# 16-head attention rebuilt on two score layouts, with stacked operands sent through DRAM

## The chip, the cores and the metric

The kernel runs on one core of a Trainium2 chip. The metric is the device time of one execution in microseconds; lower is better.

## The reference

Four layers, each an attention and a feed-forward part, on x of 16 x 256 tokens by 128. The attentions of layers 0, 2 and 3 have 16 heads of width 8 over a context of 64 rows per batch, and are what is changed:

```python
x = x + xattn(_layernorm(x), ctx)
# in xattn: q, k, v by head
scores = jnp.einsum('bhqd,bhkd->bhqk', q, k)
scores = jnp.where(mask, NEG, scores)          # layer 0: keys whose token is 0
probs = jax.nn.softmax(scores / np.sqrt(HD), axis=-1)
attn = jnp.einsum('bhqk,bhkd->bhqd', probs, v)
return attn @ Wo + bo
```

Layers 2 and 3 have a mask of query by key, which with these inputs masks nothing. Layer 1's attention has one head and is not touched.

## The kernel before, in words

Tokens lie on partitions: 32 tiles of 128 tokens, two tiles to a batch. `X` holds the residual stream in SBUF for the whole kernel, `MV` its mean and variance per token.

Before each attention a preparation (`prep_parts`, L196) computes the keys transposed, `KT`, and `VB`, the values padded with a column of ones. It is a stage of its own for layers 0 and 3; for layer 2 it runs at the end of the expert stage, just before the rows that the experts wrote are gathered back to `XH` by indirect DMAs on GpSimd (L1668) and added to `X` (L1644).

`mha` (L334) is one stage. Each engine has its own instruction list, made by `tile_slots` (L184) of one slot per tile, written out for the first and last four and in a loop of four slots between; engines meet at semaphores alone, and each executes its own list in order. In a slot:

- TensorE computes the scores of tile t+1 in two halves (`scores`, L388): queries stationary, and as moving operand `kbd`, the keys spread over 16 heads with zeros elsewhere, 512 columns a half, in f32. Between the halves it transposes the 8 chunks of the exponentials of tile t-1 (L407). Then come the transpose of the attended tile t-3 (L417), the attended values of tile t-2 (L425: 8 products with the transposed exponentials stationary and 18 columns moving) and the output projection of t-3 (L431). In layer 0 each half gets a bf16 product more, for the padding mask (L396).
- VectorE divides tile t-3 by its sums (L528, L531), and for each half of t+1 takes the maximum of each head (L518) and writes the shifted scores `Z` (L521). It adds the output of t-4 to `X` and takes its statistics (L542 to L551).
- ScalarE takes the exponential (L457), copies the transposed exponentials out of PSUM (L462) and the smaller transposes (L445, L450, L469).
- GpSimd builds `kbd` (L484) and adds the output bias (L486), once per batch.

There is no DMA within an attention stage, beyond the last of the loads that were issued earlier.

## Time and profile before

| | us |
|---|---|
| median of 3 runs | 1820.06 (1814.22 to 1820.89) |
| the profiled execution | 1815.55 |
| its span in the trace | 1813.7 |
| attention of layer 0, 35.2 to 237.5 | 202.3 |
| attention of layer 2, 989.2 to 1165.0 | 175.8 |
| attention of layer 3, 1589.3 to 1764.5 | 175.2 |
| TensorE busy | 1415.0 (78%) |
| VectorE busy | 1143.6 (63%) |
| ScalarE busy | 616.5 (34%) |
| GpSimd busy | 265.5 (15%) |

The span is what the trace covers; the execution's own time has 1.85 us more around it. The attention stages are measured from the first reciprocal of the token scales (L142) to the last statistics. A busy TensorE is one whose records follow each other without a gap; a record contains some 0.17 us in which the next has already begun. The granted clock (PEclk) is 1.00 where TensorE is granted 2.4 GHz, and 0.50 at 1.2 GHz.

### The profile page before, as it was taken

The page shows a single profiled execution, that of the slowest core. Times are in us where ns is not written, and L with a number is a line of the kernel's source. Part 1 is how long each engine was busy: PE and PEld are TensorE (multiplying, and loading weights), DVE is VectorE, ACT ScalarE, POOL GpSimd, SP SyncE. Part 2 cuts the span into 40 slices and gives each one's busy share as a digit, 9 for nine tenths or more (in the row PEclk, how much of TensorE's full clock was granted, in tenths as well). Part 3 has the DMA queues.
Part 4 walks back from the last instruction along what each step waited for, and adds up shares of the span by engine and source line. Part 5 has one row for each costly group of instructions (what it writes and reads, how often), then busy time and mean ns, then how long its engine had stood idle before and what let it go on. Part 6 is the DMA issues. An engine that isn't in the chain of part 4 may idle for free. (4 is left out here: it accounts for less than half of the span.)

```text
span 1813.7 us, 26829 instructions
## 1 busy us (share of the span) xinstructions
PE 1415.0 (78%) x7716; PEld 1061.2 (59%) x7749; DVE 1143.6 (63%) x3741; ACT 616.5 (34%) x1055; POOL 265.5 (15%) x237
## 2 busy tenths in 40 slices
PE   3999976999976663302760999699999999789982
PEld 1666665998964453201540777567777777557761
DVE  5777774576647875670243888645556655578868
ACT  1444403444433220000110555334444444345541
POOL 1222100010101100064246222000000000032202
PEclk8999986999995555555875999799999999989995
DMA  6000000000000031002321000000000000000001
GB/s 218 1 0 0 0 1 1 1 2 0 1 1 1 0 124 30 0 20 84 113 69 32 1 0 0 1 1 1 1 1 0 0 0 1 1 1 0 0 1 47
DMA packets 38579, 34.21 MB, mean 19 GB/s; under 512 B 8672, under 2 KB 35552, under 8 KB 38112
## 3 DMA queue, kind: packets, MB, share of 16 engines
q1 hardware_dynamic: 35168, 26.78, 4.9%
q0 software_dynamic: 3328, 6.43, 1.1%
q8 instruction: 39, 0.64, 0.1%
q14 instruction: 44, 0.36, 0.1%
HBM read 24.15 MB, written 9.44 MB: 19 GB/s over the span
## 5 line engine op out<-in xcount | busy, mean ns | idle before, releaser
L392 PE MATMUL mha_pS<-mha_kbd,mha_qT 128*128 128x512 f32 x384 | 203.9, 616 | 3.6 <-ACT mha_qT L450 3.4
L484 POOL TENSOR_TENSOR mha_kbd<-KT,w_ctx 128x1024 f32<-128x1024 f32 x48 | 91.2, 1901 | 758.3 <-SPq L97 460.5
L1982 DVE SCALAR_TENSOR_TENSOR tree_hl<-tree_pH,tree_hh 128x512 fp32r<-128x512 f32 x192 | 132.4, 689 | 94.8 <-ACT tree_hh L1879 93.2
L425 PEld LDWEIGHTS mha_pO<-VB,mha_PT 128*128 128x128 f32 x1536 | 183.2, 192 | 10.8 <-issue 8.7
L425 PE MATMUL mha_pO<-VB,mha_PT 128*128 (+1 forms) x1536 | 178.3, 259 | 0.0
L1879 ACT ACTIVATE tree_hh<-tree_pH 128x512 fp32r<-128x512 f32 x192 | 114.6, 597 | 146.1 <-PE tree_pH L1783 112.1
L518 DVE TENSOR_REDUCE mha_nm<-mha_pS 128x8 f32<-128x512 f32 x192 | 131.6, 686 | 44.4 <-PE mha_pS L396 24.1
L521 DVE TENSOR_TENSOR mha_Z<-mha_pS,mha_nm 128x512 f32<-128x512 f32 x192 | 132.9, 692 | 19.3
L462 ACT ACTIVATE mha_PT<-mha_pT 128x1024 f32<-128x1024 f32 x96 | 98.3, 1024 | 136.5 <-PE mha_pT L407 136.0
L457 ACT ACTIVATE mha_PR<-mha_Z 128x1024 f32<-128x1024 f32 x96 | 101.5, 1057 | 86.1 <-DVE mha_Z L521 86.0
L407 PEld LDWEIGHTS mha_pT<-w_ctx,mha_PR 128*128 128x128 f32 x768 | 87.4, 141 | 38.4 <-issue 38.2
L1796 PE MATMUL tree_pY<-tree_hh,w2h 128*128 128x512 f32 x192 | 101.0, 526 | 5.5 <-DVE tree_hl L1982 5.2
L1124 ACT ACTIVATE ffn_hid<-ffn_pH,w_ffn 128x512 f32<-128x512 f32 x128 | 85.5, 687 | 54.3 <-PE ffn_pH L1049 53.7
L407 PE MATMUL mha_pT<-w_ctx,mha_PR 128*128 128x128 f32 x768 | 101.2, 275 | 0.0
L1233 DVE SCALAR_TENSOR_TENSOR ffn_acc<-ffn_pE,ffn_wt,ffn_acc 128x128 f32<-128x128 f32 x192 | 54.1, 344 | 71.1 <-PE ffn_pE L1062 71.0
L1062 PEld LDWEIGHTS ffn_pE<-W2R,ffn_hid 128*128 128x128 f32 x768 | 93.6, 192 | 4.4
L1062 PE MATMUL ffn_pE<-W2R,ffn_hid 128*128 128x128 f32 x768 | 93.8, 275 | 0.0
L1780 PE MATMUL tree_pH<-tree_xTh,w1h 128*128 128x512 f32 x192 | 80.8, 421 | 1.0 <-DVE tree_sel L1976 1.0
L1569 PE MATMUL exp_pX<-w_ctx,exp_xe 128*128 128x128 f32 (+1 forms) x48 | 12.2, 336 | 84.5 <-DMA exp_xe<-slots_in 84.5
L1782 PE MATMUL tree_pH<-tree_xTh,w1l 128*128 128x512 f32 x192 | 76.6, 399 | 0.0
L1796 PE MATMUL tree_pY<-tree_hl,w2h 128*128 128x512 f32 x192 | 76.2, 397 | 0.0
L1781 PE MATMUL tree_pH<-tree_xTl,w1h 128*128 128x512 f32 x192 | 76.1, 396 | 0.0
(422 smaller groups left out, 2822.8 us busy)
## 6 DMA issues: line engine op xcount, KB each, us to landing
w_tree_full<-in_tree_full_dram SPq DMA_DIRECT2D x1, 4224.0 KB, 14.2
exp_W<-in_L_W_dram SPq DMA_DIRECT2D x32, 128.0 KB, 2.3
slots_in<-route_zero SPq DMA_DIRECT2D x40, 64.0 KB, 1.8
w_rot<-in_rot_dram SPq DMA_DIRECT2D x1, 2307.0 KB, 8.7
X<-in_x_dram SPq DMA_DIRECT2D x8, 256.0 KB, 5.8
exp_xe<-slots_in SPq DMA_DIRECT2D x16, 128.0 KB, 3.0
slots_out<-exp_ye POOLq DMA_DIRECT2D x16, 128.0 KB, 2.9
out_dram<-X SPq DMA_DIRECT2D x8, 256.0 KB, 2.3
```

The lines of the kernel that those rows point to most:

```text
L392: ins = pe.matmul(pS[:, n, :], qT[u][:, P * v:P * v + P], kbd[u][:, 8 * n:8 * n + 8, :], start=True, stop=not key_mask)
L407: ins = pe.transpose(pT[:, P * c:P * c + P], PR[v][:, P * c:P * c + P], ident)
L425: ins = pe.matmul(pOv[:, c, :], PT[v][:, P * c:P * c + P], VB[:, a.b(-2), c, :], start=True, stop=True)
L457: act.activation(PR[v][:], Z[v][:].rearrange("p h k -> p (h k)"), ACT.Exp, scale=HD ** -0.5).then_inc(s["P"], 1)
L462: act.activation(PT[v][:], pT[:], ACT.Copy).then_inc(s["PT"], 1)
L484: pool.tensor_tensor(kbd[u][:], kb, bmask.unsqueeze(2).to_broadcast([P, H, SK]), ALU.mult).then_inc(s["kbd"], 1)
L518: dve.tensor_reduce(mx, sc, AX.X, ALU.max, negate=True).then_inc(s["nm"], 1)
L521: dve.tensor_tensor(Z[v][:, HH * n:HH * n + HH, :], sc, mx.unsqueeze(2).to_broadcast([P, HH, SK]), ALU.add).then_inc(s["Z"], 1)
L1062: ins = pe.matmul(pE[p % 2][:, j, :], hc, core.W2R[:, P * r:P * r + P], start=(c == 0), stop=(c == 1))
L1796: ins = pe.matmul(bank[:], w2[:, k0], h[k % 2][:], start=(c == 0 and i == 0), stop=False)
L1879: act.activation(hh[k % 2][:], pH[k % 2][:], ACT.Relu).then_inc(s["h"], 1)
L1982: dve.scalar_tensor_tensor(hl[k % 2][:], pH[k % 2][:], 0.0, hh[k % 2][:], ALU.max, ALU.subtract).then_inc(s["lo"], 1)
```

## The change

Each attention computes its scores twice. In the first layout (tokens on partitions) they serve only to find the maximum of each head. In the second (keys on partitions) they are computed again with the maximum taken off inside the product, so that the exponential is taken straight out of PSUM into the layout that the attended values need. `Z`, its subtraction and the 8 transposes of the exponentials per tile are gone.

All score products are in f32r. To keep the precision, queries and keys are split into a high and a low part, stacked on partitions: in four groups of four heads, query rows high, high, low against key rows high, low, high, 32 rows each. Below these lie rows of ones, and 8 rows with the negated maxima (high and low part) of the group. The queries of four tiles (a quad) are written to DRAM as `qd` and read back stacked (2 writes and 3 reads of 256 KB each per quad, 8 quads); the maxima of a batch go the same way as `md` (32 KB each way, 16 batches). SyncE issues all of these in one list.

The attended values have `VB` stationary (18 columns) and 256 columns of exponentials moving, four products into the partitions from 0, 32, 64 and 96 of one PSUM bank, two such sets per batch. Their result is copied to `OT` and transposed back to tokens on partitions (`tokens`, 2 transposes per tile).

All slots are written out, from -8 to 44; slot t takes the scores and maximum of tile t, the second scores and exponentials of tile t-6, the attended values of t-8, the division (`rc`, `at`), transpose and projection of t-11, and the residual addition of t-12. VectorE's list takes `largest(t)` first in its slot. The normalisation of `X` moves to ScalarE. The preparation makes the stacked keys `KS` from 8 products with a copy on ScalarE and a subtraction on VectorE for each, where it had 2 products and copies; it also fills the extra rows. GpSimd spreads `KS` over the heads (`ks`), 1024 columns per batch, as it did for `kbd`.

The core of the diff (the declarations, the branch for a mask that masks something, and the packing of the inputs are left out):

```diff
+            for g in range(NQ):
+                need(pe, s_l, NQ * n + g - 1)
+                pe.matmul(pk[g % 2][0:3 * HR, :], w("wk3")[:, 3 * HR * g:3 * HR * g + 3 * HR], ctx, start=True, stop=True).then_inc(s_k, 1)
...
+            for g in range(NQ):
+                act.wait_ge(s_k, NQ * n + g + 1)
+                act.activation(KS[0:3 * HR, g, 512 * n:512 * n + 512], pk[g % 2][0:3 * HR, :], ACT.Identity,
+                               bias=w("bk3")[0:3 * HR, g:g + 1]).then_inc(s_kt, 1)
...
+        dve.memset(KS[3 * HR:last, :, :].bitcast(F32), 1.0).then_inc(s_z, 1)
         dve.memset(VB[:], 0.0).then_inc(s_z, 1)
-        dve.wait_ge(s_z, 1)
+        if key_mask:
+            dve.wait_ge(s_z, 1)
+            dve.tensor_scalar(KS[3 * HR:3 * HR + 3, :, :], core.itok[3 * HR:3 * HR + 3, :].unsqueeze(1).to_broadcast([3, NQ, B * SK]), 0.0,
+                              core.w("mha0", "neg3")[3 * HR:3 * HR + 3, :], ALU.is_equal, ALU.mult)
+        lo = slice(HR, 2 * HR)
+        for n in range(2):
+            for g in range(NQ):
+                dve.wait_ge(s_kt, NQ * n + g + 1)
+                kl = KS[lo, g, 512 * n:512 * n + 512]
+                dve.scalar_tensor_tensor(kl, pk[g % 2][lo, :], w("bk3")[lo, g:g + 1], kl, ALU.add, ALU.subtract).then_inc(s_l, 1)
+        dve.wait_ge(s_z, 2)
...
+    QB, KB, QT = 3, 4, 4
+    QS = QT * P
+    SC = HD ** -0.5
...
+        PT = [core.XH[:, 16 * u:16 * u + 16, :].rearrange("p (c t) d -> p c (t d)", c=CH) for u in range(2)]
+        OT = two("OT", [P, 2, S])
...
+        pS = st.ps("pS", [P, H, SK])
+        pST = st.ps("pST", [P, CU, S])
+        pQ, pO, pAb, pYb = (st.ps(n, [P, 512]) for n in ("pQ", "pO", "pA", "pY"))
+        pOv = pO[:].rearrange("p (r t) -> p r t", r=2)
+        pA, pV = pAb[:, 0:P], pAb[:, P:P + S]
+        pVc = pV.rearrange("p (c w) -> p c w", w=HR)
+        pY, pN = pYb[:, 0:P], pYb[0:2 * H, P:P + S]
...
+        FIRST, LAST = -8, T + 13
+        UN, AT, OE, HT = 6, 8, 10, 11
+        quad = lambda t: t // QT
...
+            def write_queries(q):
+                sp.wait_ge(s["q"], q + 1)
+                for n, src in enumerate((qh, ql)):
+                    sp.dma_start(core.qd[n, q], plain(src[:])).then_inc(s["qw"], 16)
+            def read_queries(q):
+                u = q % QB
+                sp.wait_ge(s["qw"], LW * (q + 1))
+                need(sp, s["ST"], QT * (q - QB) + QT)
+                for n, h in enumerate((0, 0, 1)):
+                    sp.dma_start(plain(qs[u][HR * n:HR * n + HR, :, :]), core.qd[h, q].rearrange("(g r) c -> r g c", g=NQ)).then_inc(s_ld[u], 16)
+            def write_shifts(b):
+                sp.wait_ge(s["nT"], b + 1)
+                sp.dma_start(core.md[b], plain(nT[b % 2][:])).then_inc(s["mw"], 16)
+            def read_shifts(b):
+                u, c0 = (b // 2) % QB, S * (b % 2)
+                sp.wait_ge(s["mw"], 16 * (b + 1))
+                need(sp, s_m[b % 2], 16 * (b // 2))
+                sp.dma_start(plain(qs[u][K0:K1, :, c0:c0 + S]), core.md[b].rearrange("(g j) c -> j g c", g=NQ)).then_inc(s_m[b % 2], 16)
+            for t in range(FIRST, LAST):
+                if not even(t) and live(t - 3):
+                    write_shifts((t - 3) // TB)
+                if t % QT == 3 and live(t + 5):
+                    write_queries(quad(t + 5))
+                if not even(t) and live(t - 3):
+                    read_shifts((t - 3) // TB)
+                if t % QT == 2 and live(t + 2):
+                    read_queries(quad(t + 2))
...
+            def scores(t):
+                b, q = t // TB, quad(t)
+                u, c0 = q % QB, P * (t % QT)
+                if t % QT == 0:
+                    pe.wait_ge(s_ld[u], LD * (q // QB + 1))
+                if even(t):
+                    pe.wait_ge(s["k"], b + 1)
+                need(pe, s["nm"], t)
+                for g in range(NQ):
+                    ins = pe.matmul(pS[:, NH * g:NH * g + NH, :], qs[u][0:KC, g, c0:c0 + P], ks[b % KB][0:KC, g, :, :],
+                                    start=True, stop=True)
                 ins.then_inc(s["S"], 1)
...
+            def shifts(b):
+                pe.wait_ge(s["nx"], b + 1)
+                need(pe, s["X"], TB * b + 2 - HT)
+                need(pe, s["nT"], b)
+                for v in range(TB):
+                    src = nx[b % 2][:, v, :, :, :].rearrange("p g n h -> p (g n h)").bitcast(F32)
+                    ins = pe.transpose(pN[:, P * v:P * v + P], src, ident)
+                ins.then_inc(s["nTp"], 1)
+            def scores_T(b, i):
+                u, c0 = (b // 2) % QB, S * (b % 2)
+                if i == 0:
+                    pe.wait_ge(s_m[b % 2], LM * (b // 2 + 1))
+                need(pe, s["P"], TB * b + i)
+                for n in range(CU):
+                    c = CU * i + n
+                    g, h0 = c // 2, 2 * (c % 2)
+                    ins = pe.matmul(pST[:, n, :], ks[b % KB][0:K1, g, h0:h0 + 2, :], qs[u][0:K1, g, c0:c0 + S], start=True, stop=True)
+                ins.then_inc(s["ST"], 1)
+            def attend(b, r):
+                if r == 0:
+                    need(pe, s["OT"], b)
+                pe.wait_ge(s["P"], TB * b + 2)
+                for j in range(4):
+                    c = 4 * r + j
+                    ins = pe.matmul(pOv[HR * j:HR * j + VW, r, :], VB[:, b, c, :], PT[b % PB][:, c, :], start=True, stop=True)
+                ins.then_inc(s["O"], 1)
+            def tokens(t):
+                b, v = divmod(t, TB)
+                pe.wait_ge(s["OT"], b + 1)
+                need(pe, s["aT"], t)
+                for r in range(2):
+                    ins = pe.transpose(pV[:, P * r:P * r + P], OT[b % 2][:, r, P * v:P * v + P], ident)
+                ins.then_inc(s["V"], 1)
+            def heads_T(t):
+                pe.wait_ge(s["at"], t + 1)
+                pe.transpose(pA, at[:], ident).then_inc(s["aTp"], 1)
+            def output(t):
+                pe.wait_ge(s["aT"], t + 1)
+                need(pe, s["X"], t)
+                need(pe, s["nT"], min(B, (t + HT) // TB))
+                pe.matmul(pY, aT[t % 2][:], w("wo"), start=True, stop=True).then_inc(s["Y"], 1)
...
+            for t in range(FIRST, LAST):
+                if live(t):
+                    scores(t)
+                if live(t - UN):
+                    scores_T((t - UN) // TB, (t - UN) % TB)
+                if live(t - HT):
+                    heads_T(t - HT)
+                if live(t - AT):
+                    attend((t - AT) // TB, (t - AT) % TB)
+                if even(t) and live(t - 2):
+                    shifts((t - 2) // TB)
+                if live(t - HT + 1):
+                    tokens(t - HT + 1)
+                if t % QT == 1 and live(t + 7):
+                    x_transposes(quad(t + 7))
+                if t % QT == 2 and live(t + 6):
+                    queries(quad(t + 6))
+                if live(t - HT):
+                    output(t - HT)
...
+            def q_evac(q):
+                act.wait_ge(s["qp"], q + 1)
+                need(act, s["qw"], LW * q)
+                act.activation(qh[:], pQ[:], ACT.Identity, bias=w("bq")).then_inc(s["qh"], 1)
+            def shifts(b):
+                act.wait_ge(s["nTp"], b + 1)
+                need(act, s["mw"], 16 * (b - 1))
+                act.activation(nT[b % 2][:], pN, ACT.Copy).then_inc(s["nT"], 1)
+            def exponentials(b, i):
+                n = TB * b + i
+                act.wait_ge(s["ST"], n + 1)
...
+                need(act, s["O"], TB * (b - PB) + 2)
+                act.activation(PT[b % PB][:, CU * i:CU * i + CU, :], pST[:], ACT.Exp, scale=SC).then_inc(s["P"], 1)
...
+            for t in range(FIRST, LAST):
+                if even(t) and live(t - OE):
+                    attended((t - OE) // TB)
+                if live(t + 10) and t + 10 >= QT:
+                    normalise(t + 10)
+                if live(t - HT):
+                    heads_T(t - HT)
+                if live(t - UN):
+                    exponentials((t - UN) // TB, (t - UN) % TB)
+                if even(t) and live(t - 2):
+                    shifts((t - 2) // TB)
+                if t % QT == 1 and live(t + 7):
+                    x_evac(quad(t + 7))
+                if t % QT == 2 and live(t + 6):
+                    q_evac(quad(t + 6))
...
+                def q_low(q):
+                    dve.wait_ge(s["qh"], q + 1)
+                    dve.scalar_tensor_tensor(ql[:], pQ[:], w("bq"), qh[:], ALU.add, ALU.subtract).then_inc(s["q"], 1)
+                def largest(t):
+                    dve.wait_ge(s["S"], t + 1)
...
+                    dve.tensor_reduce(nm[:, t, :], pS[:], AX.X, ALU.max, negate=True).then_inc(s["nm"], 1)
+                def split_shift(b):
+                    dve.wait_ge(s["nm"], TB * b + 2)
+                    need(dve, s["nTp"], b - 1)
+                    src = nm[:, TB * b:TB * b + TB, :].rearrange("p v (g h) -> p v g h", h=NH)
+                    dve.tensor_copy(nx[b % 2][:, :, :, 0, :], src).then_inc(s["nh"], 1)
+                    dve.wait_ge(s["nh"], b + 1)
+                    dve.tensor_tensor(nx[b % 2][:, :, :, 1, :], src, nx[b % 2][:, :, :, 0, :], ALU.subtract).then_inc(s["nx"], 1)
...
+                for t in range(FIRST, LAST):
+                    if live(t):
+                        largest(t)
+                    if live(t - HT):
+                        r = t - HT
+                        dve.wait_ge(s["V"], r + 1)
+                        dve.reciprocal(rc[r % 2][:], pVc[:, :, 2 * HD:VW]).then_inc(s["rc"], 1)
+                    if even(t) and live(t - 2):
+                        split_shift((t - 2) // TB)
+                    if live(t - HT):
                         need(dve, s["aTp"], r)
...
+                        dve.wait_ge(s["rc"], r + 1)
+                        dve.tensor_tensor(at[:].rearrange("p (c h d) -> p c h d", h=2, d=HD),
+                                          pVc[:, :, 0:2 * HD].rearrange("p c (h d) -> p c h d", d=HD),
+                                          rc[r % 2][:].unsqueeze(3).to_broadcast([P, CH, 2, HD]), ALU.mult).then_inc(s["at"], 1)
+                    if live(t - HT - 1):
+                        x = t - HT - 1
+                        dve.wait_ge(s["Y"], x + 1)
+                        dve.wait_ge(s["bo"], x // TB + 1)
+                        dve.tensor_tensor(X[:, x, :], pY, X[:, x, :], ALU.add).then_inc(s["X"], 1)
+                    if live(t - HT - 1):
+                        dve.wait_ge(s["X"], x + 1)
+                        dve.bn_stats(bn[x % 2][:], X[:, x, :]).then_inc(s["bn"], 1)
...
+                    if t % QT == 2 and live(t + 6):
+                        q_low(quad(t + 6))
+                    if live(t - HT - 1):
+                        dve.wait_ge(s["bn"], x + 1)
+                        dve.bn_aggr(MV[:, x, :], bn[x % 2][:])
...
+            if key_mask:
+                for u in range(QB):
+                    dve.memset(qs[u][3 * HR:K0, :, :].bitcast(F32), 1.0).then_inc(s["one"], 1)
+            dve.memset(pO[:], 0.0).then_inc(s["zero"], 1)
             rs_dve(dve)
+            dve.scalar_tensor_tensor(NB[:], MV[:, :, 0], -1.0, RS[:], ALU.mult, ALU.mult).then_inc(s["nb"], 1)
...
```

## Rows read from the trace of the kernel before

**Rows 1.** Windows over the attention stages: window, length, PE, PEld, DVE, ACT, POOL, PEclk, DMA, GB/s.

```profile
35.20:237.50 202.30, 196.13 (x1120) 128.46 (x1120) 144.06 (x357) 88.63 (x129) 39.18 (x32) 0.97 0.00 0
989.20:1165.00 175.80, 166.80 (x1056) 128.23 (x1056) 136.69 (x357) 86.32 (x130) 39.36 (x32) 0.96 0.00 0
1589.30:1764.50 175.20, 167.46 (x1056) 128.44 (x1056) 136.88 (x357) 86.46 (x130) 39.23 (x32) 0.96 0.00 0
```

**Rows 2.** Timeline in layer 3's attention, one slot and more: start us, us, instruction.

```profile
1661.14 1.02 PE L392 MATMUL mha_pS<-mha_kbd,mha_qT 128*128 128x512 f32 x2
...
1662.00 1.04 PE L407 MATMUL mha_pT<-w_ctx,mha_PR 128*128 128x128 f32 x8
...
1664.06 1.86 PE L425 MATMUL mha_pO<-VB,mha_PT 128*128 x16
...
1665.77 0.47 PE L431 MATMUL mha_pY<-w_mha,mha_aT 128*128 128x128 f32 x2
...
1666.07 1.02 PE L392 MATMUL mha_pS<-mha_kbd,mha_qT 128*128 128x512 f32 x2
...
1666.17 0.25 DVE L528 RECIPROCAL mha_rc<-mha_pO 128x16 f32<-128x16 f32 x1
...
1666.53 0.29 DVE L531 TENSOR_TENSOR mha_at<-mha_pO,mha_rc 128x128 f32<-128x128 f32 x1
...
1668.78 0.60 PE L386 MATMUL mha_pQ<-mha_xT,w_mha 128*128 128x256 f32 x2
```

**Rows 3.** Groups of instructions, layer 3's attention, 1610 to 1700: busy us, mean ns.

```profile
L518 DVE TENSOR_REDUCE mha_nm<-mha_pS 128x8 f32<-128x512 f32 x36 | 24.5, 681 | 2.2 <-PE mha_pS L392 2.2
...
L484 POOL TENSOR_TENSOR mha_kbd<-KT,w_ctx 128x1024 f32<-128x1024 f32 x10 | 19.0, 1902 | 56.4 <-PE mha_pS L392 56.4
...
L462 ACT ACTIVATE mha_PT<-mha_pT 128x1024 f32<-128x1024 f32 x18 | 18.4, 1024 | 22.8 <-PE mha_pT L407 22.8
...
L542 DVE TENSOR_TENSOR X<-mha_pY,X 128x128 f32 x17 | 4.8, 281 | 0.0
```

**Rows 4.** Timeline of TensorE in layer 2's tree stage: two f32r products.

```profile
1315.76 0.40 PE L1781 MATMUL tree_pH<-tree_xTl,w1h 128*128 128x512 f32 x1
1315.99 0.40 PE L1782 MATMUL tree_pH<-tree_xTh,w1l 128*128 128x512 f32 x1
```

**Rows 5.** Timeline at the start of layer 3's attention.

```profile
1589.80 0.19 DVE L143 TENSOR_TENSOR mha_nta<-mha_vea,RS 128x32 f32<-128x32 f32 x1
1590.02 0.19 DVE L144 TENSOR_TENSOR mha_nta<-mha_nta,RS 128x32 f32<-128x32 f32 x1
...
1591.81 0.69 PE L381 MATMUL mha_pQ<-w_ctx,mha_xh 128*128 128x128 f32 x2 [7.56 <-DVE mha_xh L501]
...
1592.97 1.22 PE L386 MATMUL mha_pQ<-mha_xT,w_mha 128*128 128x256 f32 x2 [0.47 <-ACT mha_xT L445]
```

**Rows 6.** DMA issues on the page: size of each, median us from issue to landing.

```profile
X<-in_x_dram SPq DMA_DIRECT2D x8, 256.0 KB, 5.8
...
out_dram<-X SPq DMA_DIRECT2D x8, 256.0 KB, 2.3
```

**Rows 7.** Timeline: preparation of layer 3, of layer 0, and the gather before layer 2.

```profile
1579.23 1.98 DVE L216 MEMSET VB<- 128x2304 f32 x1 [0.82 <-PEq L97]
...
1579.85 0.69 ACT L213 ACTIVATE KT<-prep_pk,w_mha 128x512 f32<-128x512 f32 x1 [3.64 <-PE prep_pk L206]
...
1581.60 0.61 DVE L227 TENSOR_TENSOR VB<-prep_pv,w_mha 64x64 f32<-64x64 f32 x4
...
14.86 0.73 DVE L292 TENSOR_SCALAR nbias<-itok,w_mha 3x1024 bf16<-3x1024 int32 x1
...
968.14 0.75 DVE L1644 TENSOR_TENSOR X<-X,XH 128x512 f32<-128x512 f32 x1 [3.73 <-DMA XH<-slots_out,slots]
```

**Rows 8.** Windows elsewhere: layer 1's attention, and the expert stage (columns as in Rows 1).

```profile
548.00:600.00 52.00, 34.74 (x104) 21.34 (x104) 41.67 (x278) 15.06 (x40) 6.52 (x9) 0.51 0.00 1
...
882.00:886.00 4.00, 1.83 (x5) 1.19 (x6) 0.57 (x2) 0.00 (x0) 1.26 (x2) 0.73 0.67 203
```

385 lines of the change are left out of this document (147 added, 238 removed).

## The prediction

> **What bounds the kernel now.** Two views say where the change can act. The windows over the three attention stages come first [rows 1]: 202.3, 175.8 and 175.2 us, 553.3 of the span's 1813.7. TensorE is busy for 95 to 97% of each at a granted clock of 0.96 to 0.97, and VectorE for 144.1, 136.7 and 136.9 us, ScalarE for half of the time. The timeline of one slot shows how tightly TensorE is packed [rows 2]: from one first half of scores (1661.14) to the next (1666.07) pass 4.93 us, in which 8 transposes (1.04), the attended values (1.86), the projection (0.47) and the two halves of scores follow each other. So before, these stages are bound by TensorE's own work: 32 slots of some 5.0 us make 160, and filling and emptying the pipeline 16. In layer 0 two mask products per tile lengthen the slot; from 202.3 - 16 it is 5.8 us.
>
> The change therefore has to be priced as a slot: what one tile costs once the new pipeline is full, and what the longer pipeline costs before and after that. All sums below are against the profiled execution, 1815.6 us; the median of the runs, 1820.1, is 4.5 above it.
>
> **The new slot, step by step.** What TensorE is spared is clear: the two halves in f32, 1.9 us of issue, and the 8 transposes. An f32r product of 512 columns starts 0.23 us before the next [rows 4]; one of 256 columns is then 0.12, and the two layouts together are 8 of these, 0.96 us. VectorE loses the subtraction into `Z`. But the order of the two lists makes a loop that the old kernel did not have. In slot t TensorE issues the scores of t, then those of t-6, and then `heads_T(t-11)`, which needs `at(t-11)`. VectorE has the sums for that from the slot before, yet its list puts `largest(t)` first, and that waits for the scores of this very slot. So TensorE stands still after its second scores until VectorE has taken the maximum and divided. Counting from the start of slot t:
> - Four score products: the last starts at 0.36 and ends 0.12 + 0.17 later, at 0.65. The 0.17 is what a record holds beyond its issue: 0.40 against 0.23 [rows 4].
> - `largest`: 512 PSUM elements take 0.68 and 128 take 0.28 [rows 3], so 1.04 ns an element, and 1024 take 1.22; I take 1.24. With 0.03 before it.
> - `rc` and `at`: `at` starts 0.36 after `rc` and takes 0.29 [rows 2], 0.65. In even slots `split_shift` stands between, two small operations that follow at 0.22 each as two such ones do [rows 5]: 0.45 in half of the slots, 0.22 in the mean.
> - With 0.07 for the hand-over, `heads_T` starts at 2.86. TensorE's second scores were issued by 0.96; it has been idle for 1.7 us.
> - From there TensorE issues: `heads_T` 0.12 (8 transposes take 1.04), attended values A, `shifts` 0.22 every second slot, `tokens` 0.24, x transposes 0.48 and queries 0.92 every fourth, the projection 0.30 (1665.77 to 1666.07) [rows 2]. That is 0.12 + 0.11 + 0.24 + 0.12 + 0.23 + 0.30 + A, 1.12 + A.
> - Two hold-ups more. `q_low` is ahead of the next `largest` on VectorE: a query product (0.92 + 0.17), its copy (0.69 for 512 columns [rows 7]) and `q_low` (0.69) end 0.8 us after the next scores would have been ready, every fourth slot: 0.20. And `output` must wait in even slots until ScalarE has copied the shifts out of the same bank, which stands behind the exponential of 1024 columns, 1.02 [rows 3]; where no query product covers that it is 0.5 us, every fourth slot: 0.12.
>
> The slot is 2.86 + 1.12 + 0.20 + 0.12 + A = 4.30 + A.
>
> **A is the open price**: four f32 products of 256 columns whose outputs lie in four different 32-partition strips, which no row shows. Bounds: one after the other each costs 0.43, from 0.60 for a product of 256 columns less 0.17 [rows 2], so A = 1.72; all four at once, A = 0.45. An f32 product is two records, and the second of a product writes where its first does. If it must wait for that and only neighbours of different products overlap, there are five steps of 0.215 where there were eight: A = 1.07. I take this one: it is the middle of the ends, and the rows are as far from both, since none of them writes part of the partitions.
>
> So the slot is 5.37 us, against 5.0 in layers 2 and 3 and 5.8 in layer 0.
>
> **Fill and drain.** Only slots 11 to 31, 21 of them, are full. Before slot 0 come normalisation, transposes, queries and their two copies at the half clock: a transposition of two is 0.69 and a product of 256 columns 1.22 [rows 5], and with 512 columns everywhere this ends at 8 us; then two writes and three reads of 256 KB. A store of that size lands in 2.3 us and a load among many in 5.8 [rows 6]; I take 3 and 5, and scores start at 16.5 us, with 10 and 20 as ends. Slots 0 to 7 are chains of scores, maximum and the next scores, 1.95 us, with 0.7 more in even slots and 2.7 more where queries come: 23 us. Slots 8 to 10 add the attended values: 10. Slot 11 begins at 50. After slot 31 there are six slots of 2.2, two of 1.8, five of 1.3 and an end of 1.3: 24.5. A layer is 50 + 21 x 5.37 + 24.5 = 187.3, three are 562, 9 more than 553.3.
>
> **Preparation.** VectorE fills `KS`: 4096 columns at the 1.98 us of 2304 [rows 7] are 3.5, before everything else. Then eight rounds of product, copy (0.69) and subtraction (0.69) over two banks: two rounds take about 2.5 us, 10 in all, less what the fills cover, and only then come the additions into `VB` (0.61 for four). Layer 3's preparation grows by 12.5. Layer 0's grows as much, its mask rows (four times 0.73) standing for the removed multiplication of `KT`, and its attention begins with three fills of 2048 columns, 5.3, of which 0.5 hides beside the table load: 4.8. For layer 2 I charge nothing: the same 12 us lie ahead of additions to `X` that each wait 3.73 us for a gather [rows 7]; seven such waits absorb them. Without that cover it would be 12.
>
> **Costed at nothing otherwise**: ScalarE has 1.02 + 0.3 + 0.3 + 0.3 + 0.5 = 2.4 us of work in a slot of 5.3. GpSimd builds 1024 columns per batch as before, 1.90 us [rows 3], in two slots. The queue of SyncE carries 1.3 MB in 21 us; the queries are asked for three slots, 15 us, before use, the shifts come back after one write and one read, 5 us, and have three slots. SyncE's list is in order: a late `q` would hold up the shifts behind it, but it is there 1.3 us into the slot.
>
> **The clock.** In a stretch of the expert stage in which TensorE was idle for over half of the time the granted clock was 0.73, and in layer 1's attention, 34.7 busy of 52, it was 0.51 [rows 8]; before it was 0.96. With 1.7 us idle in each slot I take 0.95 of what it is at 1.00 for the 2.8 us that TensorE has on the path: 63 x 2.8 / 0.95 less 63 x 2.8, 9 us.
>
> Sum: 1815.6 + 9 + 12.5 + 12.5 + 4.8 + 9 = **1863 us**. TensorE loses its work and gets a wait for VectorE instead.
>
> **The rivals.**
> - *The strips run one after the other* (A = 1.72). For it: each f32 product in the rows before, even of 18 columns, has its own 0.12 [rows 2], none overlap. Slot 6.00; 29 slots have attended values, so 3 x 29 x 0.65 = 57 more, less 1 for the smaller wait of `output`: 1919.
> - *All four strips at once* (A = 0.45), not slower than before. The slot loses 0.62, but `output` then waits on the exponential and the shift copy in every even slot, 0.33 instead of 0.12 in the mean: 4.96. Drain gives 5 us a layer. 3 x (21 x 0.41 + 5) = 41 less: 1822, no change. It decides as soon as A is below 0.5; if the fill is 5 us a layer shorter as well, 1807, and faster when measured. The Trainium skill's page "TensorE: Matmul & The Clock Gate", section "Part 3: Packing small matmuls — row/col tiling", is for it: matmuls in different column strips run concurrently, a few ns apart. By that rule the sum is the 1822 of this rival; no row of the trace has such strips.
> - *The clock stays low.* If TensorE is granted 0.5 as in layer 1's attention, its 2.8 us on the path double: slot 8.2, 3 x 21 x 2.8 = 176 less the 9 counted: 2030. For it: the stages start at half clock and each slot has a gap. Against: the old stages start at half clock too and still had 0.96 in the mean [rows 1]. It decides from a mean clock below 0.9.
> - *The order costs nothing*: `at` is ready before TensorE asks. Then the slot is TensorE's sum, 0.96 + 1.07 + 1.12 = 3.15, or VectorE's 1.24 + 0.87 + 0.03 and some 1.1 for `X`, the statistics and `q_low`, 3.3, with the hold-ups 3.6, and 3 x 21 x 1.77 = 111 go: 1752. Against it is the list itself.
>
> **How the numbers follow.** Forecast 0.40, strips in sequence 0.22, strips at once 0.20, low clock 0.08, order free 0.10. A measurement of this kernel tells from no change what is over 0.5%, 9 us. The forecast's own range, with fill at its ends (-6 to +4 a layer) and clock 0.9 to 1.0, is 1836 to 1887. Of the rival at 1822, which its fill moves either way, half is faster, as is the case of a free order, and a little of the forecast: faster 0.24. Same 0.13, from the other half; slower 0.63. The range takes in both neighbours and some error of the fill: 1795 to 1930.
>
> **What would show it.** Right: TensorE idle for about 1.7 us before `heads_T`, released by `at`; `largest` at 1.24; slots of 5.4 us; scores of slot 0 some 15 us after the token scales; preparations of about 21 us. Wrong: starts of the four strip products 0.43 apart, or 0.02 apart; a clock under 0.9; TensorE waiting on the stacked reads in the steady state; or no wait for `at` at all.

## The result, and the profile after

The kernel after takes 1901.3 us (median of four runs, 1893.8 to 1908.1) against 1820.5 for the kernel before beside it: a ratio of 1.044 (95% interval 1.039 to 1.050). Its profiled execution took 1908.1 us, the slowest of the four, with a span of 1906.1 against 1813.7. Of 92.4 us more in the span, the attention stages hold 33.4, and what comes ahead of them 56.1:

| stretch | change, us | forecast |
|---|---|---|
| start and preparation of layer 0 | +20.1 | +17.3 |
| attention of layer 0 | -10.9 | -15.0 |
| expert stages with layer 2's preparation | +20.6 | 0 |
| attention of layer 2 | +21.3 | +11.5 |
| preparation of layer 3 | +15.4 | +12.5 |
| attention of layer 3 | +23.0 | +12.1 |
| the rest | +2.9 | 0 |

(An attention runs from the reciprocal of its token scales to its last statistics. The expert row runs from the token scales of the feed-forward part behind layer 0's attention, and layer 3's preparation from those of layer 2's tree stage, each to the token scales of the attention that follows. The forecast of an attention stage is 187.3 less the old length; its 9 us for the clock stand for all three together.)

First the three attention stages, answering to [rows 1], and then the full slots alone, from the maximum of tile 11 to that of tile 31, 20 slots each. The columns are window, length, PE, PEld, DVE, ACT, POOL, PEclk, DMA, GB/s.

```profile
55.30:246.70 191.40, 131.25 (x752) 86.43 (x752) 85.80 (x238) 75.44 (x145) 37.87 (x31) 0.71 0.23 61
1019.30:1216.40 197.10, 136.10 (x752) 89.85 (x752) 85.97 (x238) 75.77 (x146) 37.83 (x31) 0.68 0.22 59
1658.20:1856.40 198.20, 139.68 (x752) 91.65 (x752) 85.84 (x238) 75.66 (x145) 37.85 (x31) 0.65 0.22 59
...
112.40:216.80 104.40, 73.09 (x456) 50.37 (x457) 49.43 (x142) 39.09 (x76) 24.48 (x20) 0.78 0.21 57
1078.70:1186.30 107.60, 77.90 (x456) 53.72 (x457) 49.40 (x141) 39.32 (x76) 24.45 (x20) 0.72 0.20 56
1714.80:1827.70 112.90, 84.26 (x456) 57.17 (x457) 49.46 (x142) 39.45 (x76) 24.50 (x20) 0.64 0.19 53
```

TensorE was busy for 95 to 97% of these stages and is now for 69 to 70%, and the granted clock fell from 0.96 or 0.97 to between 0.65 and 0.71: in long stretches TensorE is granted 1.2 GHz and not 2.4. A full slot is 5.22, 5.38 and 5.64 us, longest where the clock is lowest. One slot of layer 0 shows the loop that the prediction described:

```profile
135.29 0.33 PE L471 MATMUL mha_pA<-w_ctx,mha_at 128*128 128x128 f32 x1 [1.65 <-DVE mha_at L631]
135.55 0.63 PE L458 MATMUL mha_pO<-XH,VB 128*18 128x256 f32 x8
136.11 0.50 PE L466 MATMUL mha_pA<-w_ctx,mha_OT 128*128 128x128 f32 x2
...
136.69 1.20 PE L428 MATMUL mha_pS<-mha_ks,mha_qs 99*128 99x256 f32 x4
137.69 1.05 PE L449 MATMUL mha_pST<-mha_qs,mha_ks 107*128 107x256 f32 x4
137.93 1.23 DVE L590 TENSOR_REDUCE mha_nm<-mha_pS 128x16 f32<-128x1024 f32 x1 [1.96 <-PE mha_pS L428]
139.07 0.25 DVE L625 RECIPROCAL mha_rc<-mha_pA 128x16 f32<-128x16 f32 x1
139.50 0.28 DVE L631 TENSOR_TENSOR mha_at<-mha_pA,mha_rc 128x128 f32<-128x128 f32 x1
139.84 0.48 PE L471 MATMUL mha_pA<-w_ctx,mha_at 128*128 128x128 f32 x1 [1.09 <-DVE mha_at L631]
140.25 1.06 PE L458 MATMUL mha_pO<-XH,VB 128*18 128x256 f32 x8
```

VectorE stands still for 1.96 us until the scores are there, takes the maximum, then divides, and TensorE waits for `at` (the bracket gives the idle time and who ended it). In all TensorE waits for `at` 93.8 us in 78 of 96 slots, 1.2 us each in the mean where the forecast had it idle for 1.7. Two things differ from the forecast's slot: the four score products are 1.0 us apart in all and not 0.48, since they run at half clock, and the eight records of attended values (L458) give way to the next work 0.56 us after their first start at full clock (135.55 to 136.11) and after 0.98 at half (140.25 to 141.23), not after 1.07. In the trace's single records the first records of the four products start 0.007 us apart, and the second ones follow 0.21 us later.

Layer 2's preparation lies in the expert stage. Its row of before shows VectorE held by the gather's arrivals, 3.73 us each [rows 7]; after, it is late itself:

```profile
944.32 3.47 DVE L192 MEMSET KS<- 8x4096 f32 x1 [0.91 <-issue]
...
962.03 0.61 DVE L214 TENSOR_TENSOR VB<-exp_pX,w_mha 64x64 f32<-64x64 f32 x4
967.77 0.61 DVE L214 TENSOR_TENSOR VB<-exp_pX,w_mha 64x64 f32<-64x64 f32 x4 [5.13 <-remote]
978.32 0.61 DVE L214 TENSOR_TENSOR VB<-exp_pY,w_mha 64x64 f32<-64x64 f32 x4 [9.94 <-remote]
991.65 0.61 DVE L214 TENSOR_TENSOR VB<-exp_pY,w_mha 64x64 f32<-64x64 f32 x4 [12.72 <-remote]
...
1001.28 0.67 DVE L1742 TENSOR_TENSOR X<-X,XH 128x512 f32<-128x512 f32 x1
```

VectorE waits 27.8 us for the sixteen value products, which by TensorE's own records ran from 960.0 to 963.7, while GpSimd issues gathers from 947.2 to 988.6. The first addition to `X` comes at 1001.3, 54 us after the first gather is issued; the kernel before had it at 950.2, 11 us after the first gather.

### The profile page after: what moved, and what is told of

Same layout as the page of the kernel before. It is cut to its first block and busy times, and to the rows that moved or that the text cites. A ratio compares the mean times of both kernels' runs of the same rounds, so it can differ in the third digit from the quotient of the medians.

```text
span 1906.1 us, 22929 instructions
## 1 busy us (share of the span) xinstructions
PE 1316.9 (69%) x6776; PEld 949.0 (50%) x6809; DVE 1019.5 (53%) x3414; ACT 594.0 (31%) x1121; POOL 261.2 (14%) x237
## 5 line engine op out<-in xcount | busy, mean ns | idle before, releaser
L590 DVE TENSOR_REDUCE mha_nm<-mha_pS 128x16 f32<-128x1024 f32 x96 | 117.2, 1220 | 192.1 <-PE mha_pS L428 192.1
L568 POOL TENSOR_TENSOR mha_ks<-KS,w_ctx 104x1024 fp32r<-104x1024 f32 (+1 forms) x48 | 90.8, 1892 | 904.2 <-POOLq L99 553.2
L428 PE MATMUL mha_pS<-mha_ks,mha_qs 96*128 96x256 f32 (+1 forms) x384 | 107.6, 423 | 35.0 <-DMA mha_qs<-queries 14.1
L428 PEld LDWEIGHTS mha_pS<-mha_ks,mha_qs 96*128 96x128 f32 (+1 forms) x384 | 82.5, 291 | 53.1 <-issue 26.1
L530 ACT ACTIVATE XH<-mha_pST 128x1024 f32<-128x1024 f32 x96 | 97.9, 1020 | 14.1 <-PE mha_pST L449 13.7
L449 PE MATMUL mha_pST<-mha_qs,mha_ks 104*128 104x256 f32 (+1 forms) x384 | 82.7, 352 | 2.1 <-ACT XH L530 1.3
L458 PE MATMUL mha_pO<-XH,VB 128*18 128x256 f32 x768 | 76.5, 479 | 0.0
L449 PEld LDWEIGHTS mha_pST<-mha_qs,mha_ks 104*128 104x128 f32 (+1 forms) x384 | 73.6, 263 | 4.2 <-issue 2.3
L1894 PE MATMUL tree_pY<-tree_hh,w2l 128*128 128x512 f32 x192 | 75.2, 392 | 0.0
L471 PE MATMUL mha_pA<-w_ctx,w_top 128*128 128x128 f32 x64 | 24.3, 380 | 61.4 <-DVE w_top L631 61.4
```

What stands on the lines that cost most here:

```text
L428: ins = pe.matmul(pS[:, NH * g:NH * g + NH, :], qs[u][0:KC, g, c0:c0 + P], ks[b % KB][0:KC, g, :, :], start=True, stop=True)
L449: ins = pe.matmul(pST[:, n, :], ks[b % KB][0:K1, g, h0:h0 + 2, :], qs[u][0:K1, g, c0:c0 + S], start=True, stop=True)
L530: act.activation(PT[b % PB][:, CU * i:CU * i + CU, :], pST[:], ACT.Exp, scale=SC).then_inc(s["P"], 1)
L568: pool.tensor_tensor(ks[b % KB][0:K1, :, :, :], kb, hb, ALU.mult).then_inc(s["k"], 1)
L590: dve.tensor_reduce(nm[:, t, :], pS[:], AX.X, ALU.max, negate=True).then_inc(s["nm"], 1)
L1894: ins = pe.matmul(bank[:], w2[:, k0], h[k % 2][:], start=(c == 0 and i == 0), stop=False)
```

## The experiments

All times are medians of four runs; each ratio is to the kernel before on the same chip, which took 1816.0 to 1816.9.

**1. The order alone: `at` before the maximum.**

```
-                    if live(t):
-                        largest(t)
                     if live(t - HT):      # rc, split_shift, at
...
+                    if live(t):
+                        largest(t)
                     if live(t - HT - 1):  # X, statistics
```

> One edit to the kernel after: in each slot VectorE does the reciprocal, the split of the shifts and the division (at) for tile t-11 before it takes the maximum of tile t. Theory of the order (TensorE stands still before heads_T because at is behind the newest maximum): heads_T finds at ready, the wait of TensorE for at goes, and a full slot is TensorE's own sum or VectorE's, 3.6 us at full clock and about 4.2 us at the clocks seen after (0.65 to 0.76), where it was 5.2 to 5.6. Over 63 full slots that is 75 to 115 us less than after, 1785 to 1825 us. Rival (the low clock is what makes the slot, and the wait for at only lies where TensorE would be slow anyway): slots stay above 5.0 us, the time stays above 1875 us, and the wait for at is replaced by another of the same length.

Measured: 1758.0 us, ratio 0.969 (0.965 to 0.973), 137 us under the kernel after by the ratios, more than the theory allowed. The full slots of the three layers:

```profile
106.80:175.00 68.20, 55.54 (x456) 37.47 (x457) 53.70 (x141) 40.13 (x76) 24.02 (x20) 1.00 0.33 88
1021.30:1089.60 68.30, 55.53 (x456) 37.57 (x457) 53.80 (x141) 40.20 (x76) 24.01 (x20) 1.00 0.32 87
1608.50:1677.10 68.60, 55.95 (x456) 37.54 (x457) 54.01 (x142) 40.13 (x76) 24.06 (x20) 1.00 0.32 87
```

The slot is 3.42 us, the wait for `at` 19.7 us in 27 slots, and the granted clock 1.00 without anything else having been done to it. The kernel before's time is beaten by 59 us by moving two lines, and the forecast's rival of a free order, 1752, was near. So the order costs the kernel after its whole loss and more, but this run does not say how much of it is the standing still and how much the half clock that comes with it.

**2. The clock alone: busy work in the wait, order unchanged.**

```
+                if live(t - HT) and live(t):
+                    need(pe, s["nT"], min(B, (t - 1) // TB))
+                    need(pe, s["X"], t - HT - 1)
+                    for _ in range(5):
+                        pe.matmul(pYb[:, 3 * P:4 * P], ident, ident, start=True, stop=True)
                 if live(t - HT):
                     heads_T(t - HT)
```

(Beside these lines: in the same slots VectorE's addition to `X` also waits for the transposition behind these products.)

> The kernel after with the order left alone, but in each of the 21 full slots TensorE issues five f32 products of the identity (128 columns, into unused columns of the bank of the projection) just before it waits for at; X's addition waits until the transposition behind them is done, so that nothing is read meanwhile. They change no result and fill most of the idle 1.7 us. Theory that the clock is a cause of its own: granted clock of the full slots rises from 0.64 to 0.76 to 0.9 or more, the four score products of one layout from 1.2 us to about 0.6, the full slot from 5.2 to 5.6 to about 4.9, and the time falls by 20 to 45 us against after. Rival (the slot is VectorE's chain, the clock costs next to nothing in it): the clock rises and the slot stays within 0.1 us, time within 10 us. Third way: the five products are too few to move the clock; then they only lengthen the slot or change nothing.

Measured: 1844.9, ratio 1.016 (1.012 to 1.020), 52 us under the kernel after. Windows of the full slots, and TensorE in one of layer 3:

```profile
111.40:201.90 90.50, 77.72 (x652) 59.56 (x651) 51.19 (x142) 38.83 (x76) 24.47 (x20) 1.00 0.25 67
1056.80:1147.30 90.50, 77.84 (x653) 59.74 (x652) 51.20 (x141) 38.90 (x76) 24.50 (x20) 1.00 0.25 67
1675.00:1765.90 90.90, 77.82 (x652) 59.80 (x652) 51.23 (x142) 38.83 (x76) 24.51 (x20) 1.00 0.24 66
```
```profile
1720.10 0.72 PE L428 MATMUL mha_pS<-mha_ks,mha_qs 96*128 96x256 f32 x4
1720.66 0.64 PE L449 MATMUL mha_pST<-mha_qs,mha_ks 104*128 104x256 f32 x4
1721.15 1.28 PE L491 MATMUL mha_pY<-w_ctx 128*128 128x128 f32 x10
1722.71 0.33 PE L471 MATMUL mha_pA<-w_ctx,w_top 128*128 128x128 f32 x1 [0.28 <-DVE w_top L636]
```

Useless products make the kernel faster: the clock is 1.00, a group of score products takes 0.72 instead of 1.20, and the slot falls to 4.53 us. They are not in the way: TensorE still waits for `at` in 78 slots, 37.0 us in all. With the two runs the mean slot of 5.41 splits: 0.88 is the clock, 1.11 (4.53 less 3.42) the order at full clock, and 3.42 the work. The theory's clock cause holds, at somewhat over its size.

**3 and 6. Do the strips run side by side?** Neighbours write the same 32-partition strip instead of four different ones, first on the kernel after, then on experiment 1.

```
-                for j in range(4):
-                    c = 4 * r + j
-                    ins = pe.matmul(pOv[HR * j:HR * j + VW, r, :], ...
+                for k in range(4):
+                    j, q = 2 * r + k // 2, k % 2
+                    c = 4 * q + j
+                    ins = pe.matmul(pOv[HR * j:HR * j + VW, q, :], ...
```

> The kernel after, with the 8 attended-value products of a batch issued in another order: each pair of neighbours writes the same 32-partition strip (first and second half of the bank) instead of four neighbours writing four strips. Same products, same results, same waits. If the four strips run beside each other, as the trace of after suggests (four products in 0.55 us at full clock, 1.0 at half), the four now take two to three steps one after the other: 0.9 to 1.3 us at full clock and up to twice that at half clock, the slot grows by 0.4 to 1.2 us, and the time by 25 to 90 us against after. If what made them short was something else (f32 products of 256 columns that are cheap in any order), the time stays within 5 us of after.

> The first experiment's order (at before the maximum, full slots at granted clock 1.00) with the eight attended-value products of a batch issued so that neighbours write the same 32-partition strip. In the kernel after, this edit left the time alone, but its clock rose from 0.64 to 0.78 to 0.84 to 0.89 with it, which can have paid for longer products; here the clock is full in either case. If the four strips run at once in the order of the change, the four products of a slot now take 0.9 to 1.3 us instead of 0.55, and the slot grows by 0.3 to 0.7 us, 18 to 45 us in 63 slots: 1776 to 1803. If the order of the strips does not matter, the time stays within 5 us of 1758.

On the kernel after it was inconclusive: 1908.5, ratio 1.052 (1.048 to 1.057), and the granted clock of the full slots rose to between 0.84 and 0.89, so that a longer product and a better clock can have cancelled. On experiment 1, 1766.9, ratio 0.973 (0.970 to 0.976), 9 us more. There the clock is 1.00 either way, and TensorE's timelines can be compared: four products in different strips (experiment 1) and in pairs of the same strip (experiment 6).

```profile
1643.26 0.63 PE L458 MATMUL mha_pO<-XH,VB 128*18 128x256 f32 x8
```
```profile
131.70 1.05 PE L459 MATMUL mha_pO<-XH,VB 128*18 128x256 f32 x8
```

0.42 us more for the same four products: different strips run at once, and products into the same strip do not, or only in part. The eight single records start in pairs 0.22 us apart in experiment 6, and as two groups of four 0.22 us apart in experiment 1. The slot grew by only 0.03 us of these 0.42, less than I expected, since TensorE is not what bounds it (experiment 5); the emptying of the pipeline, where it is, grew by about 2 us a layer.

**4 and 8. Layer 2's stall: fewer waits, fewer signals.** On the kernel after, one wait for all sixteen value products; on experiment 1, one signal for four.

```
-            for n in range(4):
-                dve.wait_ge(s_v, 4 * n + 4)
+            if h == 0:
+                dve.wait_ge(s_v, B)
+            for n in range(4):
```
```
-            pe.matmul(pv[b // 4]...).then_inc(s_v, 1)
+            ins = pe.matmul(pv[b // 4]...)
+            if b % 4 == 3:
+                ins.then_inc(s_v, 1)
```

> The kernel after, with the preparation's four waits of VectorE on the value products, before each group of additions into VB, made one wait for all sixteen products before the first addition. In the trace of after, layer 2's preparation has stalls of 5.1, 9.9 and 12.7 us at these waits, long after the products were done, while GpSimd issues the 32 gathers; before, they were in front of the gather and took 0.3 us. If each wait meets the cost by itself (a wait during the gather's issue is slow), one wait leaves one stall of 5 to 13 us or none, VectorE's preparation ends 15 to 28 us earlier, the additions to X are hidden behind the gather again, and the time falls by 12 to 22 us against after. Rival (VectorE itself is held up by GpSimd in that stretch, whatever it executes, through the memory port they share): the stall moves to the additions, and the time stays within 5 us.

> The first experiment's order, and in the preparation TensorE signals VectorE after every fourth value product instead of after each. The stalls in layer 2's preparation grow from wait to wait (5.1, 9.9, 12.7 us in the kernel after), as if each of TensorE's signals took 1 to 3 us to arrive. If that is so, a quarter of the signals leaves a quarter of the stalls, 20 us become 5, and the time falls by 5 to 15 us to 1743 to 1753. If the stalls are of the stretch and not of the signals (the products themselves or VectorE being held up until the gathers have been issued), they stay, and the time stays within 5 us of 1758.

Measured: 1901.1, ratio 1.048 (1.044 to 1.052), the same as the kernel after; and 1756.4, ratio 0.967 (0.964 to 0.971), the same as experiment 1. The stall of experiment 4 is one, and those of experiment 8 are a little shorter than experiment 1's 3.1, 6.5 and 10.6:

```profile
962.75 0.17 DVE L208 MEMSET VB<- 64x128 f32 x1 [0.19 <-issue]
982.00 1.13 DVE L215 TENSOR_TENSOR VB<-exp_pX,w_mha 64x64 f32<-64x64 f32 x8 [19.09 <-remote]
...
986.91 0.25 DVE L215 TENSOR_TENSOR VB<-exp_pY,w_mha 64x64 f32<-64x64 f32 x1
988.27 0.23 DVE L215 TENSOR_TENSOR VB<-exp_pY,w_mha 64x64 f32<-64x64 f32 x1 [1.11 <-issue]
988.99 0.23 DVE L215 TENSOR_TENSOR VB<-exp_pY,w_mha 64x64 f32<-64x64 f32 x1 [0.48 <-issue]
```
```profile
917.42 0.61 DVE L216 TENSOR_TENSOR VB<-exp_pX,w_mha 64x64 f32<-64x64 f32 x4 [1.36 <-PE exp_pY L179]
925.18 0.61 DVE L216 TENSOR_TENSOR VB<-exp_pY,w_mha 64x64 f32<-64x64 f32 x4 [7.15 <-remote]
934.31 0.61 DVE L216 TENSOR_TENSOR VB<-exp_pY,w_mha 64x64 f32<-64x64 f32 x4 [8.52 <-remote]
```

Neither the number of waits nor that of signals is the cause; both of my accounts by counting fall. Experiment 4's rival has a part in it: from 986.9 to 993.2 additions that wait for no product come with gaps of 0.46 to 1.17 us between them, so there VectorE itself is held up.

The semaphore events kept in the trace place the rest. In experiment 8 the four updates of the value products' semaphore come at 914.50, 917.40, 925.16 and 934.29, while by the records the products end at 914.48, 915.38, 916.27 and 917.16. VectorE starts 0.02 us after each of the last three. So the lateness is there when the semaphore is updated, and VectorE adds nothing to it.

**7. Value products before the key products**, on experiment 1: in `on_tensor` the loop over `pv` moves ahead of the loop over `pk`.

> The first experiment's order, and in the preparation of keys and values TensorE makes the sixteen value products before the eight key products. With one wait in place of four the stall of VectorE in layer 2's preparation stayed, as one of 19.1 us that ended at the same place in GpSimd's gathers. If what is late is the semaphore of the value products when they are made while GpSimd issues gathers (they were made 13 to 16 us into it), they are now made before it, the three stalls (3.1, 6.5 and 10.6 us in the first experiment) go, VectorE's preparation ends some 15 us earlier, hidden behind the gather, and the time falls by 5 to 15 us to 1743 to 1753. If VectorE is held up whatever it waits for, the stalls appear at the subtractions for the keys or the additions, and the time stays within 5 us of 1758.

Measured: 1738.6, ratio 0.957 (0.954 to 0.961), 19 us less than experiment 1. There is no stall, and the additions to `X` begin at 926.9 instead of 951.5 and wait for the gather's arrivals again:

```profile
911.44 1.60 DVE L203 SCALAR_TENSOR_TENSOR KS<-exp_pH,w_mha,KS 32x512 fp32r<-32x512 f32 x2 [1.05 <-ACT KS L185]
913.23 0.17 DVE L208 MEMSET VB<- 64x128 f32 x1 [0.19 <-issue]
913.41 1.14 DVE L214 TENSOR_TENSOR VB<-exp_pX,w_mha 64x64 f32<-64x64 f32 x8
...
926.87 0.67 DVE L1742 TENSOR_TENSOR X<-X,XH 128x512 f32<-128x512 f32 x1
...
945.55 0.69 DVE L1742 TENSOR_TENSOR X<-X,XH 128x512 f32<-128x512 f32 x1 [1.71 <-DMA XH<-slots_out,slots]
```

The stretch from the token scales of the feed-forward part behind layer 0's attention to those of layer 2's attention is 705.9 us, against 707.7 before and 728.3 after. Experiments 1, 2, 3 and 5, with the preparation unchanged, have 723.0 to 727.5, experiment 1 itself 723.2. So the value products' place, 13 us into the gathers' issue instead of ahead of it, is worth 17.3 us. In experiment 7 all sixteen updates of the value products' semaphore come 0.01 us after the records' ends. Why they come so late beside the gathers is open: the key products' updates in the same stretch were not late, and no run tells whether the products themselves ended later than their modelled records or only their updates were late.

**5. The maximum last**, behind the addition to `X` and its statistics too.

> The first experiment's order (at before the maximum) with one step more: VectorE also adds the projection of tile t-12 to X and takes its statistics before the maximum of tile t. In the trace of the first experiment VectorE still waits 0.5 us for the scores in most slots while these two operations (0.28 and 0.29 us) stand behind the maximum and ahead of the next reciprocal, and a slot is 3.42 us. Theory: the slot is VectorE's chain of at, maximum, X and statistics, so filling the wait takes 0.2 to 0.4 us from each of 63 slots, 13 to 25 us from the 1758, 1733 to 1745. Rival: TensorE's own sum (55.5 busy of 68.3 us in 20 slots) and GpSimd's building of the keys set the slot; the wait moves to TensorE, and the time stays within 5 us of 1758.

Measured: 1746.4, ratio 0.961 (0.958 to 0.965), 12 us less than experiment 1, just under the theory's 13 to 25; the slot is 3.27 instead of 3.42. VectorE's list is what bounded it. In every fourth slot `q_low` now stands out:

```profile
1641.96 0.75 DVE L580 SCALAR_TENSOR_TENSOR mha_ql<-mha_pQ,w_mha,mha_qh 128x512 fp32r<-128x512 f32 x1 [1.62 <-ACT mha_qh L517]
...
1643.40 0.33 PE L471 MATMUL mha_pA<-w_ctx,w_top 128*128 128x128 f32 x1 [1.01 <-DVE w_top L629]
```

**9. Three orders together**: 5, 7, and `q_low` behind the next slot's maximum (`t % QT == 3 and live(t + 5)` in place of `t % QT == 2 and live(t + 6)`).

> Three orders together: VectorE takes the maximum last (the fifth experiment), the preparation makes the value products first (the seventh), and q_low, the low part of a quad's queries, moves from the slot of its product to behind the maximum of the next slot. In the trace of the fifth experiment VectorE waits 1.6 us for ScalarE's copy of the queries in every fourth slot, and TensorE then waits 1.0 us for at. Theory: the steps are independent of each other, so from 1758 go the 12 of the maximum last, the 19 of the values first, and for q_low up to 1.0 us in 15 quads of three layers, 8 to 15 us: 1710 to 1722. Rival: q_low only moves its 0.75 us onto the next slot and the queries reach SyncE a slot later; then it is 1724 to 1732, and 1735 or more if the stacked queries come too late.

Measured: 1720.4, ratio 0.948 (0.944 to 0.951). From 1727 (1758 less 12 and 19) `q_low` took 7, just under the 8 to 15 expected of it; the slot is 3.22.

**10. The fills on GpSimd**, on 9: in layers 0 and 3 `KS` and `VB` are filled by GpSimd.

> The ninth experiment, and in the preparations of layers 0 and 3 GpSimd fills KS and VB in place of VectorE (layer 2's stays, since GpSimd gathers there). I priced the longer preparation by these fills and by the chain of product, copy and subtraction. If the fills are on the path, 3.5 us of KS and up to 2.0 of VB come out of either preparation, less what GpSimd is slower: 5 to 11 us less than the ninth. Rival: VectorE has to wait for GpSimd's fills before the additions into VB, or both slow down on their shared way to memory; then the time stays within 3 us of the ninth or grows.

Measured: 1715.5, ratio 0.944 (0.941 to 0.947): 5 us, the lower end of what was expected. GpSimd takes 3.51 us for `KS` where VectorE took 3.47; in layer 3 the first subtraction comes at 1507.5, 5.7 us after VectorE was free, for now it waits for ScalarE's first copy. In layer 3 the fills were on the path only by their excess over product and copy.

**11 and 12. Warming the clock at the head of the stage**: added products of the identity, on 9 and, with other counts, on 10.

```
+            warm(10)                      # 12: 6
             for t in range(FIRST, LAST):
+                if t == -5: warm(4)
+                if t == 0:  warm(10)      # 12: 24
                 if live(t):
                     scores(t)
+                if 0 <= t < 8: warm(3 if t < UN else 1)
```

> The ninth experiment, and TensorE issues f32 products of the identity into unused columns while it would stand still at the head of each attention stage: 10 before the first transposition, 4 before the second quad's, 10 before the first scores, 3 behind the scores of slots 0 to 5 and 1 behind those of slots 6 and 7. The granted clock up to slot 11 is 0.61 to 0.65 in every kernel of this order so far, and the four score products take 1.2 us there instead of 0.7. If TensorE's products at the half clock are on the chain of maximum and next scores, filling raises this clock to 0.8 or more and takes 0.5 us from each of some 8 to 11 slots and 1 to 2 us from the queries: 4 to 7 us a layer, 12 to 21 us less than the ninth. Rival: the added products stand in the way at half clock as long as they save, or the fill is set by the writes and reads of the queries: within 5 us of the ninth.

> The tenth experiment (three orders, fills on GpSimd) with the eleventh's added products, set by its trace: 6 in place of 10 before the first transposition, since ten ended 1.5 us after the first quad could have started, and 24 in place of 10 before the first scores, since the clock fell again to a half in the wait for the stacked queries and the first scores took 1.22 us as before. If the half clock in the fill is what the eleventh left over, slot 0 comes 1 to 2 us earlier than there and the scores of the first slots take 0.7 us: 4 to 6 us a layer less than the tenth, 1697 to 1705. Rival: the two savings overlap and the clock at the first scores has no weight beside the copies and transfers: 1708 to 1714.

Measured: 1714.9, ratio 0.942 (0.937 to 0.947), and 1711.9, ratio 0.942 (0.940 to 0.943). Both miss their theory. The clock up to slot 11, between 0.59 and 0.64 in experiments 9 and 10, rose to between 0.81 and 0.86, and the first scores take 0.74 in experiment 12 instead of 1.22. From the token scales to slot 11 the three layers took 48.7, 50.8 and 50.7 us in experiment 9, 49.4, 49.6 and 45.0 in 11, 49.5, 51.2 and 49.8 in 10, 47.9, 46.9 and 48.2 in 12. So the half clock is worth some 2.5 us of a fill of 50, not 4 to 6; slot 0's maximum even came 0.7 us later in the mean in 12. Of the 7.5 us that its three fills saved against 10 the medians show 3.6; the ends of the stages took 1.2 more, and where the rest went is open. Experiment 11 lies 5.5 under 9, just over its rival's bound, and 12 inside its rival's 1708 to 1714: the savings overlap. Experiment 12 has the lowest median, 104 us under the kernel before, and is level with 10 and 11 within the intervals: that the warming pays at all in the whole time is not shown.

## Why the prediction was right, and where it was wrong

**The loop.** That the maximum ahead of `at` puts TensorE behind VectorE was right, and it was what decided the sign. `largest` took 1.22 (I took 1.24), the wait is released by `at`, and from the maximum's start to `heads_T` it is 1.91 us (137.93 to 139.84) where I had 2.18, since the split fits between the reciprocal and `at`. Experiment 1 shows it by taking it away. Two of the forecast's own signs of being wrong came as well: the four strips' products start together (0.007 us apart), and the clock is under 0.9.

**The slot**, 5.37 forecast and 5.41 measured, is right by luck: two wrong terms cancel. The first is "A = 1.07. I take this one": it is 0.56 at full clock, and the rival of all four at once, with the Trainium skill's rule (page "TensorE: Matmul & The Clock Gate", section "Part 3: Packing small matmuls — row/col tiling"), was right about it; experiment 6 agrees with that rule. The argument from the middle of the ends was no argument, and [rows 2] was misread beside it: sixteen records in 1.71 us are 0.21 for a product of 18 columns, not 0.12. The second is "with 1.7 us idle in each slot I take 0.95": the granted clock was 0.64 to 0.78. That is 0.88 us of the slot, 55 us in 63 slots, where I had counted 9 in all. With *A* put right the forecast's own slot at full clock is 4.86; experiment 2, at full clock, has 4.53. The hold-ups are both in it: from a slot's scores to `heads_T` it takes 3.28 us where `q_low` stands in the list and 2.65 elsewhere, and TensorE waits for the copy of the shifts 3.4 us in 7 of layer 0's 20 full slots. The difference is mostly ahead of `heads_T`, 2.81 in the mean where I had 3.06 with `q_low`; from there to the next scores it is 1.79, and I had 1.80 (the two make 4.60, the slot from scores to scores). The low-clock rival, "decides from a mean clock below 0.9", had the cause right and its price of 2.8 us too high: it doubled a TensorE sum that held *A* at 1.07 and it took the whole slot at half clock.

**Fill and drain.** Slot 0's scores came 16.8, 19.1 and 17.1 us after the token scales (16.5 forecast), and slot 11's after 55.1, 57.4 and 54.7 where I had 50. From slot 0 to slot 8 it is 28 us, not 23: at half clock a slot of scores and maximum is 2.54 us and not 1.95. The end, from slot 32 on, is 25.6 us in the mean against 24.5. That is 20 us in three layers, and the 21 full slots give 5 more; less the 9 that I had counted for the clock, it is the 16 us by which the attention stages are over the forecast.

**Preparation.** Layers 0 and 3 cost 20.1 and 15.4 against 17.3 and 12.5: two rounds of subtraction take 2.65 to 3.6 us and not 2.5. Experiment 10 shows that the fills are not additive to the chain of copies, by which my list of 12.5 was right only in sum.

**The failed step** is "For layer 2 I charge nothing". Its cover was there, as experiment 7 shows (705.9 against 707.7), but I had only counted VectorE's work against the waits and not asked what else moves: the longer key part pushes the value products into the gathers' issue, where the last update of their semaphore came 28 us after the last record's end. That stretch holds 20.6 us of the 45 by which the profiled execution is over the forecast, 17.3 of them by experiment 7; the attention stages give 15.8, the other two preparations 5.7, the rest 2.9. The measured median, 1901.3, is 38 over the forecast, inside its range and on its side.

## What to carry to other kernels

Read each engine's list for the one operation that waits for this slot's newest result and see what stands behind it: here two lines in another order were worth 137 us. A wait on TensorE is paid twice, by the idle time and by the half clock on all that it does next to it, so price a new wait with both; if it can't be removed, filling it with useless products gives the second part back. When a hidden stretch grows, ask not only whether its cover is long enough but which of its steps now falls beside other traffic.

## What the runs showed of the hardware

Added f32 products of the identity, records of 1.28 us in each slot, brought the granted clock of the full slots from between 0.64 and 0.78 to 1.00, and a slot without the wait had 1.00 by itself with TensorE busy for 81% of it.

Two small VectorE operations slow down beside GpSimd. `split_shift`'s copy and subtraction of 32 columns each take 0.12 and 0.19 us in the kernel after; in experiment 9, where they fall beside GpSimd's building of the keys, the medians are 0.50 and 0.57, while the maximum, which reads PSUM, stays at 1.21 (1.22 in the kernel after). The timeline of experiment 1 shows both, each ending with GpSimd's operation beside it:

```profile
1657.53 1.90 POOL L568 TENSOR_TENSOR mha_ks<-KS,w_ctx 104x1024 fp32r<-104x1024 f32 x1 [4.73 <-PE mha_pST L449]
...
1659.03 0.43 DVE L596 CAST mha_nx<-mha_nm 128x32 fp32r<-128x32 f32 x1
1659.38 0.64 POOL L570 TENSOR_TENSOR X<-X,w_mha 128x256 f32<-128x256 f32 x1
...
1659.49 0.57 DVE L598 TENSOR_TENSOR mha_nx<-mha_nm,mha_nx 128x32 fp32r<-128x32 f32 x1
```

The Trainium skill's page "SBUF — State Buffer", section "SBUF: two separate sides", says that a VectorE operation with two SBUF inputs, or in a two-port mode, and one of GpSimd that reads SBUF exclude each other for a whole instruction. The subtraction has two such inputs, and its row agrees with this; the copy has one, and no run shows in which mode it works. No run here moved GpSimd's work away, so what these 0.7 us cost in every second slot is open.
